# Product 6 of the W_base stage for two pairs at once, and all four tiles of C21's low-rank rows behind product 5's last group

## The reference

```
q_emb = relu(q @ W3 + b3)
v = (n * v + v_sum) * q_emb[:, None, :]
y = relu(v @ W2 + b2)
base_out = y @ W_base + b_base
shared_out = (y @ A_s) @ B_s
gates = softmax(y @ W_router + b_router); top 2 of 6 weigh h = y @ A_r
routed_out = (h * w_per_e) @ B_r
out = x + base_out + shared_out + routed_out
```

## Time and profile before

| what | value |
|---|---|
| median of 3 runs | 1389.74 us (1389.46 to 1389.89) |
| the profiled execution's own time | 1388.26 us |
| its span | 1386.5 us |
| PE busy | 1382.0 us, 6069 instructions |
| DVE busy | 1037.3 us (75%) |
| ACT busy | 663.3 us (48%) |
| DMA | 255.63 MB, mean 184 GB/s |

### The profile page before, as it was taken

One profiled execution on the slowest core, in us unless ns is written; L12 is line 12 of the kernel. 1 busy time (PEld: TensorE's weight loads), 2 busy tenths in 40 slices (PEclk: granted clock), 3 DMA queues, 4 the chain that ended last, 5 costly groups with the idle time before them and its releaser, 6 DMA issues.

```text
span 1386.5 us, 18363 instructions
## 1 busy us (share of the span) xinstructions
PE 1382.0 (100%) x6069; PEld 1135.4 (82%) x6069; DVE 1037.3 (75%) x1700; ACT 663.3 (48%) x1209; POOL 75.2 (5%) x163
## 2 busy tenths in 40 slices
PE   9999999999999999999999999999999999999999
PEld 5888888888888888888888888888888888888887
DVE  6977777675776757867889768887777876778665
ACT  7774755647556574655554233443224432344231
POOL 2000110000000000000000000110001000010000
PEclk9999999999999999999999999999999999999999
DMA  8253835545165451545836629868575684846734
GB/s 320 66 178 113 264 124 156 176 116 172 62 177 163 120 166 58 158 150 175 293 124 175 240 94 348 312 193 273 179 257 175 203 277 164 280 158 202 241 117 157
DMA packets 151327, 255.63 MB, mean 184 GB/s; under 512 B 40416, under 2 KB 40672, under 8 KB 151232
## 3 DMA queue, kind: packets, MB, share of 16 engines
q1 hardware_dynamic: 135680, 199.75, 44.6%
q0 software_dynamic: 13680, 49.81, 11.7%
q10 hardware_dynamic: 1872, 4.89, 0.9%
HBM read 171.69 MB, written 82.71 MB: 183 GB/s over the span
## 4 chain that ended last, share of the span: by engine, by line
PE 100%; DVE 0%; DVEq 0%; issue 0%
PE ps L2786 33%; PE ps L2787 33%; PE ps L2788 33%; PE ps L2797 1%; PE ps L2812 0%; PE ps L2806 0%; DVE buf L2779 0%; DVEq L59 0%; DVE zeros L1954 0%
## 5 line engine op out<-in xcount | busy, mean ns | idle before, releaser
L2786 PE MATMUL ps<-act_hi,w_hi 128*128 128x512 f32 x1504 | 585.3, 389 | 0.0
L2788 PE MATMUL ps<-act_hi,w_lo 128*128 128x512 f32 x1504 | 585.1, 389 | 0.0
L2787 PE MATMUL ps<-act_lo,w_hi 128*128 128x512 f32 x1504 | 585.1, 389 | 0.0
L2786 PEld LDWEIGHTS ps<-act_hi,w_hi 128*128 128x128 f32 x1504 | 282.3, 188 | 59.6 <-DVE act_lo L1766 0.9
L2788 PEld LDWEIGHTS ps<-act_hi,w_lo 128*128 128x128 f32 x1504 | 282.3, 188 | 58.7
L2787 PEld LDWEIGHTS ps<-act_lo,w_hi 128*128 128x128 f32 x1504 | 282.3, 188 | 58.6
L1011 ACT ACTIVATE act_hi<-src 128x512 fp32r<-128x512 f32 x208 | 124.8, 622 | 95.9 <-PE ps L2788 91.9
L1773 DVE TENSOR_TENSOR act_lo<-src,act_hi 128x512 fp32r<-128x512 f32 x192 | 129.3, 684 | 22.1 <-ACT act_hi L1011 22.1
L1030 ACT ACTIVATE yhi<-buf 128x512 fp32r<-128x512 f32 x128 | 80.2, 626 | 81.1 <-PE ps L2788 80.6
L1841 DVE SCALAR_TENSOR_TENSOR buf<-ps,bb_sb,buf 128x512 f32<-128x512 f32 x91 | 67.2, 746 | 56.3 <-PE ps L2788 54.0
L2786 PE MATMUL ps<-act_hi,inner_w 128*128 128x512 f32 x252 | 98.1, 389 | 0.0
(11 more groups left out here) (181 smaller groups left out, 1659.8 us busy)
## 6 DMA issues: line engine op xcount, KB each, us to landing
src<-in_xT SPq DMA_DIRECT2D x224, 256.0 KB, 3.8
y_scratch<-buf SPq DMA_DIRECT2D x128, 256.0 KB, 3.2
src<-y_scratch SPq DMA_DIRECT2D x128, 256.0 KB, 5.3
inner_w<-inner_scratch POOLq DMA_DIRECT2D x63, 512.0 KB, 3.8
outT<-buf SPq DMA_DIRECT2D x115, 256.0 KB, 4.8
inner_scratch<-staged POOLq DMA_DIRECT2D x14, 512.0 KB, 5.1
wl_raw<-in_wbase SPq DMA_DIRECT2D x7, 1024.0 KB, 5.7
partner<-y_scratch POOLq DMA_DIRECT2D x12, 512.0 KB, 5.0
```

Of the source, the lines that this page charges most:

```text
L2786: nc.tensor.matmul(out, wh, a_h, start=start, stop=False, skip_group_check=onto)
L2787: nc.tensor.matmul(out, wh, a_l, start=False, stop=False, skip_group_check=onto)
L2788: return nc.tensor.matmul(out, wl, a_h, start=False, stop=stop, skip_group_check=onto)
```

## The change

Product 6 too is now made for both pairs at once, by seven inner products `RUN[e, 6]` in the odd pair (`inner(f, 0..6)` in `odd` of PE, f being that run), where the even pair's operand is kept in `partner6` by two copies on ACT (`keep_t4`). Its weights, seven sets of 512 KB, are made from a 1 MB load of W_base's quadrant during the even pair 10, rounded by ACT and DVE, stored to HBM by ACT and read back by POOL. The even pair's C21 is gathered in a buffer `acc6`, and its four stores move to the end of the odd pair. The low-rank rows of C21, which ended the groups of product 6, are now matmuls of their own (`low_rank_d`), all four behind product 5's last group, each onto bank j once `c22` has read it; `c21_of` on DVE reads the bank after that. SP loads the next pair's G21 tiles at other places. DVE's order in the odd pair is new throughout.

```diff
-        RUNS = [(e_of, n_of) for e_of in range(len(QUADS)) for n_of in ((1, 4) if e_of >= EARLY else (1,))]
+        RUNS = [(e_of, n_of) for e_of in range(len(QUADS)) for n_of in ((1, 4, 6) if e_of >= EARLY else (1,))]
         RUN = {key: r_of for r_of, key in enumerate(RUNS)}
-        FIRST_OF_TWO = tuple((e_of, 1) for e_of, n_of in RUNS if n_of == 4)
 
...
-                r = RUN[QUADS.index(g), 4]
+                r, s = RUN[QUADS.index(g), 4], RUN[QUADS.index(g), 6]
+                if g == SECOND:
+                    sp.wait_ge(bank_done, group_no(g - 1, 6, H - 1))
+                    load_quadrant(wl_raw[:, 6], Q22, wl_loaded[6])
                 load_ha(p)
                 load_hb(p)
                 load_hd(p)
...
-                for k in range(H):
-                    sp.wait_ge(lo_done, op_no(g, 6, k))
-                    load_y(p + 1, G21, k)
                 for j in range(H):
                     sp.wait_ge(c22_done, four(g, j))
                     sp.dma_start(outT[2 * p + 1, H + j], buf3[:, j, :]).then_inc(buf3_stored[j], 16)
-                for j in range(H):
-                    sp.wait_ge(c21_done, four(g, j))
-                    sp.dma_start(outT[2 * p, H + j], buf2[:, j, :]).then_inc(buf2_stored[j], 16)
+                for k in range(H):
+                    sp.wait_ge(a_ready, a_no(s, 1))
+                    load_y(p + 1, G21, k)
...
+                    for k in range(H if four_joined(g) else 0):
+                        if k < 2:
+                            sp.wait_ge(inner_lo_done, L2 * RUN[QUADS.index(g - 1), 6] + 4)
+                        else:
+                            sp.wait_ge(inner_made, made_no(RUN[QUADS.index(g - 1), 6], I4))
+                        load_y(p + 1, G21, k)
...
+            def keep_t4(e):
+
+                g = QUADS[e]
+                for q in range(2):
+                    if e == EARLY:
+                        act.wait_ge(four_stored[q], 16 * four_stores(4, q))
+                    else:
+                        act.wait_ge(inner_done, inner_no(RUN[e - 1, 6], L2 - 1, 1))
+                for h in range(2):
+                    act.wait_ge(t4_made, four(g, 2 * h + 1))
+                    at = slice(tile(G21, 2 * h), tile(G21, 2 * h + 2))
+                    kept = nc.scalar.activation(partner6[:, 2 * h:2 * h + 2, :], src[:, at, :], ACT.Copy)
+                kept.then_inc(a_ready, 1)
+
             def a_shift(e, k):
 
...
+            def six_add(e, m, jt):
+
+                r, g = RUN[e, 6], QUADS[e]
+                dve.wait_ge(inner_done, inner_no(r, m, jt))
+                bank = (A_BANKS if m % 2 == 0 else B_BANKS)[jt]
+                if m in (0, 1, 2, 5):
+                    j = jt if m < 2 else 2 + jt
+                    if m == 1:
+                        dve.wait_ge(inner_added, added_no(r, SIX_P0, jt))
+                    elif m == 5:
+                        dve.wait_ge(inner_added, added_no(r, SIX_U2, jt))
+                    else:
+                        dve.wait_ge(x21_added, four(g + 1 - NP, j))
+                    nc.vector.tensor_tensor(buf2[:, j, :], ps[:, bank, :], buf2[:, j, :], ALU.add
+                                            ).then_inc(inner_added, 1)
+                elif m == 3:
+                    dve.wait_ge(c21_done, four(g, 2 + jt))
+                    nc.vector.tensor_tensor(acc6[:, 2 + jt, :], ps[:, bank, :], acc6[:, 2 + jt, :], ALU.add
+                                            ).then_inc(inner_added, 1)
+                elif m == 4:
+                    dve.wait_ge(inner_added, added_no(r, SIX_V, jt))
+                    nc.vector.tensor_tensor(acc6[:, 2 + jt, :], ps[:, bank, :], acc6[:, 2 + jt, :], ALU.add
+                                            ).then_inc(c21_out, 1)
+                else:
+                    dve.wait_ge(c21_done, four(g, jt))
+                    nc.vector.tensor_tensor(acc6[:, jt, :], ps[:, bank, :], acc6[:, jt, :], ALU.add
+                                            ).then_inc(c21_out, 1)
+
+            def c21_of(p, j):
+
+                g = NP + p
+                bias = bb_sb[:, H + j:H + j + 1]
+                dve.wait_ge(lr_done, lr_no(p, LR_D, j))
+                if g in QUADS:
+                    dve.wait_ge(x21_added, four(p, H - 1))
+                    dve.wait_ge(buf2_stored[j], 16 * g)
+                    if g == SECOND:
+                        dve.wait_ge(inner_w_lo, 4 * L2)
+                    nc.vector.scalar_tensor_tensor(acc6[:, j, :], ps[:, j, :], bias, buf2[:, j, :], ALU.add, ALU.add
+                                                   ).then_inc(c21_done, 1)
+                else:
+                    f = RUN[QUADS.index(g - 1), 6]
+                    dve.wait_ge(inner_added, added_no(f, SIX_P1, j) if j < 2 else added_no(f, SIX_P6, j - 2))
+                    add_bank(j, bias, buf2[:, j, :], c21_done)
 
             def even1(e):
...
+                    inner_weight_low(3 * L2 + 2)
+                    inner_weight_sums(3)
                 inner_low(f, 4)
                 low(g, 5, 0)
                 low(g, 5, 1)
@@ -2585,27 +2773,38 @@
                 add_u2(f, 1)
                 inner_low(f, 5)
                 u4_add_x(p, 0)
+                if first:
+                    inner_weight_low(3 * L2 + 3)
                 u4_add_x(p, 1)
...
+                low(g + 1, 0, 1)
+                if first:
+                    inner_weight_low(3 * L2 + 6)
+                c22_of(p, 2)
+                low(g + 1, 0, 2)
+                low(g + 1, 0, 3)
                 c22_of(p, 3)
+                for j in range(H):
+                    c21_of(p, j)
+                    t1(g + 1, j)
 
             def c22_of(p, j):
                 dve.wait_ge(x22_added, four(p, j))
...
@@ -2661,29 +2862,76 @@
                 low(g, 2, H - 1)
                 lr_low_a(p)
                 for j in range(H):
+                    t4(g, j)
                     low(g, 3, j)
-                    t3(g, j)
-                    t4(g, j)
-                    if j == 0:
-                        lr_low_b(p)
                     if j > 0:
                         c11_add_low(p, j - 1)
+                for j in range(H):
+                    t3(g, j)
+                lr_low_b(p)
+                inner_low(f, 0)
+                inner_t1(f)
                 c11_add_low(p, H - 1)
+                inner_low(f, 1)
+                inner_t2(f)
+                u2_add_x(p, 0)
+                u2_add_x(p, 1)
+                six_add(e, 0, 0)
+                six_add(e, 0, 1)
+                inner_low(f, 2)
+                inner_t3(f)
+                c12_bank(p, 0)
+                u2_add_x(p, 2)
+                u2_add_x(p, 3)
+                six_add(e, 1, 0)
+                six_add(e, 1, 1)
+                inner_low(f, 3)
+                inner_t4(f)
+                c12_bank(p, 1)
+                six_add(e, 2, 0)
+                six_add(e, 2, 1)
+                inner_low(f, 4)
+                for j in range(H):
+                    low(g, 5, j)
+                c12_bank(p, 2)
+                six_add(e, 3, 0)
+                six_add(e, 3, 1)
+                inner_low(f, 5)
+                c12_bank(p, 3)
                 for j in range(H):
                     c11_add_x(p, j)
-                    low(g, 5, j)
-                    c12_bank(p, j)
-                for j in range(H):
-                    u4_add_x(p, j)
-                    u2_add_x(p, j)
-                for j in range(H):
-                    low(g, 6, j)
-                    if j == 2:
-                        lr_low_d(p)
+                six_add(e, 4, 0)
+                six_add(e, 4, 1)
+                inner_low(f, 6)
+                u4_add_x(p, 0)
+                u4_add_x(p, 1)
+                lr_low_d(p)
+                c22_of(p, 0)
+                u4_add_x(p, 2)
+                u4_add_x(p, 3)
+                c22_of(p, 1)
+                six_add(e, 5, 0)
+                six_add(e, 5, 1)
+                for j in range(H):
                     c12_add_x(p, j)
-                    if j > 0:
-                        c22_of(p, j - 1)
-                c22_of(p, H - 1)
+                c22_of(p, 2)
+                if p < LAST:
+                    low(g + 1, 0, 0)
+                    low(g + 1, 0, 1)
+                six_add(e, 6, 0)
+                six_add(e, 6, 1)
+                if p < LAST:
+                    low(g + 1, 0, 2)
+                    low(g + 1, 0, 3)
+                c22_of(p, 3)
+                c21_of(p, 0)
+                c21_of(p, 1)
+                c21_of(p, 2)
+                if p < LAST:
+                    t1(g + 1, 0)
+                    c21_of(p, 3)
+                    for j in range(1, H):
+                        t1(g + 1, j)
 
...
             def pair2(p):
                 g = NP + p
-                c21(g - 1, H - 1)
+                if not four_joined(g - 1):
+                    c21(g - 1, H - 1)
                 if g in QUADS:
```

(37 more changed lines are left out.)

309 lines of the change are left out of this document (221 added, 88 removed).

## The result

The changed kernel takes 1398.25 us (median of 5 runs, 1396.49 to 1403.21) beside 1389.46 us for the kernel before: ratio 1.0069, 95% interval 1.0050 to 1.0089. It is slower. The profiled execution took 1396.49 us with a span of 1394.7, against 1388.26 and 1386.5 before.

A forecast was written before the change was run, and what follows sets the result against it. TensorE, busy 1382.0 of 1386.5 us, bounds the kernel. Terms -9.03 + 3.8 + 7.6 + 2.5 + 0.9 + 0.4 + 0.3 = +6.5 us gave a median of 1396.2 us, 0.47% more; range 1386.5 to 1403.

The forecast's parts named there:

- The matmuls: Product 6 of two pairs takes 84 matmuls instead of 96, three times: -8.16 us.
- The last low-rank tile of C12: In odd pairs it no longer waits for ScalarE's bank copy, 0.29 us each, three times: -0.87 us.
- VectorE at the end of an odd pair: Bank reads and `t1` delay `inner_low(r, 0)`; TensorE waits 1.9 us at pairs 12 and 14: +3.8 us.
- The late transfers: C11 stores start late, so `ha_raw` lands 14.7 us into pairs 12 and 14, needed by 10.9: +7.6 us.
- it would be wrong if `ha_raw` were not the last thing that these pairs wait for: One of the stated signs against the forecast, for pairs 12 and 14; no size given.
- the first stall: TensorE's 1.9 us wait at `inner(r, 0)` of pairs 12 and 14, lengthened if VectorE reaches `c22` of bank 3 late.
- The Trainium skill's figure: HBM gives one core about 358 GB/s; 13.9 MB would take 38.8 us, each `ha_raw` stall 4.7 us.
- Pair 10: The quadrant ahead of `ha_raw` costs +2.5 us; a rounding and four sums ahead of product 5's operands +0.9.
- The small ones: Late `c11_add_low` of bank 5 at `inner(f, 0)`, three times, +0.4 us; stores at the program's end +0.3.
- 367 and 404: Burst's rate in GB/s: 367 forecast, chance 0.50; rival 404 gives 1388.9 us, 0.18 including up to about half the stalls.
- the transfers are no matter: Rival: `ha_raw` lands in time, only VectorE's stalls remain, -3.6 us, 1386.1 us; chance 0.18 with its variant.
- loads alone ran at 343: Argument against the 404 GB/s rival, from the stretch 1188 to 1213 us: the burst holds sixteen loads in a row.

The follow-up runs named there:

- h: Changed kernel with the edits of a, b, c and d, and `c11_add_low` of the last bank ahead of `inner_t1(f)`: median 1381.33 us, ratio 0.9945 to the kernel before.
- a: Changed kernel with the four `c11_add_x` of odd pairs spread one by one among the earlier inner products: median 1388.56 us, ratio 0.9993 to the kernel before.
- i: h with the edit of c taken back: median 1384.05 us, ratio 0.9964 to the kernel before.
- k: The changed kernel unedited, run and profiled again (the second profile): median 1399.71 us, ratio 1.0081 to the kernel before.
- e: Changed kernel storing half the columns of the odd pairs' and `acc6` output tiles, with as many transfers: median 1389.99 us, ratio 1.0008 to the kernel before.
- c: Changed kernel with `inner_low(r, 0)` ahead of `c21_of` bank 3 and the four `t1` at the end of odd pairs: median 1401.82 us, ratio 1.0094.
- b: Changed kernel with `ha_raw` for pairs 12 and 14 issued before the odd pair's C22 stores: median 1397.79 us, ratio 1.0062 to the kernel before.
- d: Changed kernel with pair 10's W_base quadrant issued behind its loads and four weight sums behind `low(10, 5, 3)`: median 1397.64 us, ratio 1.0060.

## Why the prediction was right, step by step

- **The matmuls**, -8.16: 36 fewer, and h shows the whole of it once the holes are closed. **The last low-rank tile of C12**, -0.87: its hole is gone in all three odd pairs.
- **VectorE at the end of an odd pair**, +3.8: right in mechanism, and in size when the crowd lets VectorE be on time (a stand of 1.84 us in a and i, where the slots give 1.83). In the changed kernel the hole was 2.2 and 2.7 us (2.0 and 2.7 in k), as VectorE came to the bank reads late: in pair 13 it waited for the load of x12, and ScalarE for that of G11, both in the crowd. The prediction had named this as what would lengthen the first stall, and put it at nothing.
- **The late transfers**, +7.6: the mechanism is shown by a (start the burst sooner), e (fewer bytes) and c (come sooner, wait longer). In pair 12's burst it took 38.5 us from the C11 store to `ha_hi`, where I had 37.9, and the burst began 52.4 us into the pair for 52.1. The size was 6.4 in one profile and 8.7 in the other. What the step lacked is that `ha_raw` was not alone: `inner_t2` waits for the stores of C21, and when it was done VectorE stood only 1.3 us more for `ha_hi` in pair 12 and 2.4 in pair 14, so that an early `ha_raw` is no cure by itself (b). The prediction had said that it would be wrong if `ha_raw` were not the last thing that these pairs wait for; it was, by no more than that.
- **The Trainium skill's figure**, "DMA: Bandwidth & Descriptors", section "Specifications", 358 GB/s for one core: the trace doesn't agree for the burst as a whole (376 GB/s over 38.5 us, and 403 over the ten us from 1043). The row gives the figure as half of a stack that two cores share, and this program runs on one. The stalls were 4.1 and 2.3 or 4.5 and 4.2 us where that figure made them 4.7 each.
- **Pair 10**, +2.5 and +0.9: 1.9 and 3.1 in the two profiles for the first, 1.0 for the second; d took both away.
- **The small ones**: +0.4 was 0.7 (0.25 a pair, not 0.13), and the end of the program +0.6 for +0.3.
- **The sum** was 1.7 us short of the profiled execution, and by the medians the change is +8.8 us where it had +6.5. What it lacked: pairs 12 and 14 together have 12.7 us of holes and slow matmuls for its 11.4 (13.5 in the second profile), and 0.7 us stand at the end of pair 13, where the last low-rank tile waits for a bank read that VectorE does late behind x12. Pair 10's first hole was 0.6 us too large in it, and the start of pair 10 came 0.9 us sooner; neither is the kernel's own, as in the second profile that hole is 0.6 us longer than forecast and pair 10 starts 0.1 us later than before. The prediction counted a stand of TensorE at its length only, and slow matmuls followed (1.4 us here, up to 4.1 in d). They don't simply add up, though. Those of the changed kernel stand in pair 14 ahead of a wait for transfers that come at their own time, and that wait is short: holes and slow matmuls there are 6.4 us, against 7.0 in k, which has none at half the clock.
- **The rivals**: the crowd as a whole ran at 376 GB/s, between the forecast's 367 and 404, but had more in it than I had counted as pieces (14.5 MB for 13.9); that the two errors meet is luck. That the transfers are no matter is refuted by a and e. The prediction's "loads alone ran at 343" is a misreading: in that stretch, 1188 to 1213, SP issued eight stores and part of four more (L776, L788 and L791 in its queue), so that none of its rows prices loads alone.

## What to carry to other kernels

When work is moved in the order of one engine, follow what its results start elsewhere: here four additions, 2.4 us of VectorE, stood 8 to 18 us later than they do in a, and twelve transfers 8 to 12 us later with them, which kept the DMA engines full at the one place where the next stage asks for its operands. When a transfer is late in a crowd, list everything that lands within some us of it, since the next gate is close behind; here it helped to start the burst sooner (a), and not to reorder it (b). And close all holes of one boundary together: with the first alone closed, TensorE only comes sooner to the next (c), and with one of two late transfers moved ahead, the other holds VectorE at the same place (b); neither gained anything.
